# A second buffer for the routed rows, a drain with its own order, and the projection's bias on GpSimd, in layer 1's attention

## The reference, cut to what matters

```python
def _L1_attn_ref(x, ...):
    ...                                   # local windows and global tokens
    mix = sigmoid(concat([local, glob]) @ gate_w + gate_b)
    out = mix * local + (1.0 - mix) * glob
    return out @ out_w + out_b            # the projection and its bias

x = x + ga * _L1_attn_ref(h, ...)         # ga: one row of 128 for each batch
h = _layernorm(x) * (1 + cb) + sb         # the rows that are routed
gout = h @ Wgate + bgate
topv, topi = top_k(gout, 2)               # each token goes to two of 8 experts
topw = softmax(topv)
x = x + gb * _L1_ffn_ref(h, ...)
```

## Time and profile before

| | |
|---|---|
| median of 3 runs | 1575.2 us (1570.2 to 1600.82) |
| profiled execution | 1568.51 us |
| its span on the core | 1566.7 us |
| mean granted TensorE clock | 0.872 |
| TensorE busy | 1236.0 us (79%) |
| VectorE busy | 883.0 us (56%) |
| GpSimd busy | 597.6 us (38%) |
| ScalarE busy | 488.4 us (31%) |

### The profile page before, as it was taken

The page is one execution under the profiler, slowest core; times in us unless marked ns, Lnnn a source line. Parts: engine busy times, 40 slices in busy tenths (PEclk is TensorE's granted clock), DMA queues, the critical chain, the costliest instruction groups (busy, mean ns, idle before and its releaser), DMA issues.

```text
span 1566.7 us, 21243 instructions
## 1 busy us (share of the span) xinstructions
PE 1236.0 (79%) x7028; PEld 722.2 (46%) x7028; DVE 883.0 (56%) x2210; ACT 488.4 (31%) x1089; POOL 597.6 (38%) x628
## 2 busy tenths in 40 slices
PE   2677777777775469965999999999993289999991
PEld 1334444444443246643456556555562145555550
DVE  3556877877875412224346666666643345656655
ACT  0222222222221135540333443344330034444340
POOL 1335654665544415554113253444235202122221
PEclk9899989988986579995799998899985599999996
DMA  6001011011011152221011111200011151111105
GB/s 260 21 0 36 21 56 36 22 55 36 28 42 44 37 212 82 77 75 58 9 30 48 33 37 41 62 22 27 27 33 34 51 155 35 34 35 36 39 21 169
DMA packets 95138, 85.25 MB, mean 54 GB/s; under 512 B 10393, under 2 KB 87578, under 8 KB 94122
## 3 DMA queue, kind: packets, MB, share of 16 engines
q1 hardware_dynamic: 86074, 65.41, 13.9%
q0 software_dynamic: 8704, 17.97, 3.6%
q10 hardware_dynamic: 256, 0.53, 0.1%
HBM read 55.40 MB, written 30.07 MB: 55 GB/s over the span
## 4 chain that ended last, share of the span: by engine, by line
PE 45%; DVE 3%; issue 3%; POOL 2%; DMA 2%; ACT 1%; SPq 1%; POOLq 0%; DVEq 0%; ACTq 0%
PE bank L1692 8%; PE bank L1934 4%; PE bank L1678 4%; PE bank L1877 3%; PE bank L1831 3%; PE bank L1702 2%; PE bank L1884 2%; PE bank L1914 2%; PE bank L1843 2%; PE bank L1903 2%; PE bank L1916 2%; PE bank L1686 2%; POOL slots L1065 1%; PE bank L1899 1%; PE bank L1948 1%
## 5 line engine op out<-in xcount | busy, mean ns | idle before, releaser
L1065 POOL DMA_INDIRECT slots<-pay,slot x128 | 134.4, 1050 | 114.9 <-issue 89.3
L1582 PE MATMUL bank<-consts,region 128*128 128x128 f32 x512 | 82.0, 310 | 110.6 <-POOL region L1102 110.6
L1080 POOL DMA_INDIRECT y<-region,xin x80 | 76.6, 958 | 195.5 <-ACT region L1309 175.2
L1582 PEld LDWEIGHTS bank<-consts,region 128*128 128x128 f32 x512 | 72.2, 214 | 156.0 <-POOL region L1102 129.0
L1692 PE MATMUL bank<-wgl,rows 128*128 x288 | 139.0, 606 | 5.8 <-ACT rows L1292 5.8
L1102 POOL TENSOR_TENSOR region<-region 128x512 f32<-128x512 f32 x64 | 83.8, 1310 | 140.5 <-DVE region L779 111.1
L913 DVE TENSOR_REDUCE rows<-bank 128x4 f32<-128x512 f32 x128 | 79.5, 683 | 84.4 <-PE bank L1831 84.4
L1292 ACT ACTIVATE rows<-bank 128x256 f32<-128x256 f32 x216 | 80.8, 382 | 102.5 <-PE bank L1686 101.5
L1080 POOL DMA_INDIRECT y<-hh,region x64 | 61.3, 957 | 117.6 <-ACT hh L1309 102.9
L640 DVE TENSOR_TENSOR rows<-bank,w0uv 128x512 f32<-128x512 f32 x72 | 49.7, 691 | 95.8 <-PE bank L1692 87.3
L1428 ACT ACTIVATE w0uv<-bank 128x512 f32<-128x512 f32 x128 | 66.1, 603 | 86.7 <-PE bank L1884 86.7
(11 more groups left out here) (306 smaller groups left out, 2660.9 us busy)
## 6 DMA issues: line engine op xcount, KB each, us to landing
xin<-slots SPq DMA_DIRECT2D x80, 65.0 KB, 1.9
region<-slots SPq DMA_DIRECT2D x64, 65.0 KB
xres<-x SPq DMA_DIRECT2D x16, 256.0 KB, 2.3
wgl<-in_wgl SPq DMA_DIRECT2D x1, 4096.0 KB, 14.3
rows<-y SPq DMA_DIRECT2D x8, 512.0 KB, 4.1
wgl<-y SPq DMA_DIRECT2D x8, 512.0 KB, 7.5
wgl<-in_x SPq DMA_DIRECT2D x8, 256.0 KB, 3.0
w0uv<-in_w0uv SPq DMA_DIRECT2D x1, 2048.0 KB
```

The costliest lines, as they stand in the source:

```text
L1065: p.indirect_dma_start(io["slots"], bass.IndirectOffsetOnAxis(ap=slot[:, k, t:t + 1], axis=0), pay[:, k, t, :], None).then_inc(S["scattere ...
L1080: p.indirect_dma_start(io["y"], bass.IndirectOffsetOnAxis(ap=xins[par][:, h, k, P + 1:P + 2].bitcast(U32), axis=0), bYs[par][:, h, k, :], ...
L1582: ins = M(bank[7][:, tile(t)], pr[:, j % 2, tile(t)], center, start=(j == 0 and t == 0), stop=(j == DH - 1 and t == NT - 1), skip_group_ch ...
```

## The change

- `pay`, `h2` and `slot` get a second copy. In layer 1 batch b uses copy b % 2; layer 0 uses copy 0 alone. `modulate(b)` in layer 1 waits until the scatter of batch b - 2 has landed (`pay_free` at NB + b, at least NB + 1), where it waited for that of b - 1.
- Steps 8 to 10 are replaced by one function `tail(t)` with t = 7 on each engine, that does the same work for the batches 5, 6 and 7 in another order. The transposes and router products of batches 6 and 7 get banks of their own (`h2_bank`, `route_bank`), so that their waits for other users of banks 4 and 5 go.
- The four products with `ones1` are removed from layer 1's projection. `obg` now holds the gated bias on all 128 partitions, and `gated_out` adds it to the rows `X` with a GpSimd operation of 128x512. `outb` is loaded broadcast over the partitions. `residual` waits for that addition.
- `maxl` now lies over weights that only layer 0 uses. Its clearing moves from the program's start to the start of layer 1's attention, and the clearing of `ones1` goes.

```diff
+        def pay_of(layer, b):
+            return pays[b % 2 if layer else 0]
@@ attention_rows
-            for i in range(-2, NB + 3):
+            for i in range(-2, NB):
                 step(i)
+            tail(LAST)
@@ VectorE
-            V.memset(ones1[:, :], 1.0).then_inc(S["prep_v"], 1)
-            V.memset(maxl[:, :, :], 0.0).then_inc(S["prep_v"], 1)
@@ residual(b)
-                v.wait_ge(S["load_k"], 32 * b + 32)
+                v.wait_ge(S["c_owg"], 3 * b + 3)
@@ modulate(b)
-                v.wait_ge(S["pay_free"], NB + b + 1)
+                v.wait_ge(S["pay_free"], max(NB + 1, NB + b))
@@ VectorE
+            def tail(t):
+                norm_local(t, 1, 1)
+                modulate(t - 1)
+                router(1, t - 2, 0.0, 0)
+                router(1, t - 2, 0.0, 1)
+                mix(t, t % 2)
+                place(1, t - 2)
+                residual(t)
+                router(1, t - 1, 0.0, 0)
+                router(1, t - 1, 0.0, 1)
+                place(1, t - 1)
+                modulate(t)
+                router(1, t, 0.0, 0)
+                router(1, t, 0.0, 1)
+                place(1, t)
@@ GpSimd, gated_out(b)
-                G_.tensor_tensor(obg[:, :], outb[:, :], mrow[0:1, M_GA, :], ALU.mult).then_inc(S["c_owg"], 1)
+                G_.tensor_tensor(obg[:, :], outb[:, :], mrow[:, M_GA, :], ALU.mult).then_inc(S["c_owg"], 1)
+                p.wait_ge(S["c_owg"], 3 * b + 2)
+                G_.tensor_tensor(X, X, bc(obg[:, :], NT, 1), ALU.add).then_inc(S["c_owg"], 1)
@@ GpSimd
+            def tail(t):
+                gated_out(t)
+                difference(t, t % 2)
+                scatter(1, t - 2, 0)
+                scatter(1, t - 2, 1)
+                ln_scale("ln2_st", "ln2_rs", t + NB)
+                normalise("c_xh2", t)
+                scattered(1, t - 2)
+                for b in (t - 1, t):
+                    scatter(1, b, 0)
+                    scatter(1, b, 1)
+                    scattered(1, b)
@@ TensorE, project
-            def project(out, src, layer):
+            def project(out, src):
                 for t in range(NT):
-                    ins = M(out[:, tile(t)], src[:, tile(t)], owg[:, :], start=True, stop=layer == 0)
-                    if layer == 1:
-                        ins = M(out[:, tile(t)], ones1[:, :], obg[:, :], start=False, stop=True)
+                    ins = M(out[:, tile(t)], src[:, tile(t)], owg[:, :], start=True, stop=True)
@@ TensorE, out(b)
-                t_.wait_ge(S["c_owg"], 2 * b + 2)
+                t_.wait_ge(S["c_owg"], 3 * b + 1)
@@ TensorE
+            def tail(t):
+                attend_local(t, 1, 1)
+                turn_out(t, 0)
+                route(t - 2)
+                turn_out(t, 1)
+                h2_T(t - 1)
+                gate(t, t % 2)
+                rank(1, t - 2)
+                out(t)
+                route(t - 1)
+                rank(1, t - 1)
+                h2_T(t)
+                route(t)
+                rank(1, t)
```

130 lines of the change are left out of this document (84 added, 46 removed).

## The result

| | before | after |
|---|---|---|
| median, us (4 runs each) | 1588.0 | 1548.7 |
| the runs, us | 1570.2, 1575.2, 1600.8, 1604.7 | 1547.9, 1548.5, 1548.9, 1552.0 |
| ratio, 95% interval | | 0.985 (0.982 to 0.989) |
| profiled execution, us (span) | 1568.5 (1566.7) | 1548.9 (1547.0) |
| mean granted clock | 0.872 | 0.874 |

The change makes the kernel faster, by 1.5% with an interval of 0.4% to either side. The profiled pair differs by 19.6 us, the medians by 39.3. Such an interval can be too narrow: in a later group of runs the kernel before, compared with itself on one chip, came out at 0.989 (0.982 to 0.996).

What follows compares the result with a forecast made beforehand. TensorE's queue was taken to bound layer 1's attention, then a drain of 81 us waiting on buffer and scatters. 9.9 + 15.3 + 0.5 = 25.7 us gave 1542.8 or 1549.5, stated as 1545, range 1531 to 1556.

Steps and rivals of the forecast that it cites:

- The chances: Whole kernel: 0.66 for a change within 2%, 0.32 for over 2% faster, 0.02 for over 2% slower.
- the sum of 25.7 us: Whole kernel: gains of 9.9 us in main steps, 15.3 in the drain and 0.5 at the start.
- Bias products, main steps: Layer 1's `out(b)`: removing length-1 products saves 1.66 us each, about 1.4 kept in four steps; 9.9 us in all.
- TensorE keeps its clock more often: Rival, main steps: two half-clock stretches of about 10 us vanish, 7 us more gained, 1536 us; chance 0.17.
- The row that spoke for it: Evidence for the clock rival: both long half-clock stretches, 10.1 and 9.9 us, begin at the removed bias products.
- The objection: Against the clock rival: in the fifth and last steps the clock falls 3 us after those products, in `attend_local`.
- The addition on GpSimd: One 128x512 addition per batch, 1.26 us, off the path: 0 us, bound 8.8; lock rival 1551 us, chance 0.07.
- The drain: After the last main step: `scatter(7)` begins at 1213.8 instead of 1229.11, limited by GpSimd's queue; 15.3 us gained.
- the order: Drain's new sequence of batches 5 to 7: counted as 2.5 us less on VectorE, within the drain's gain.
- The start: Program start: two clearings ahead of TensorE's first product go, so it starts 0.5 us earlier.
- The wait moves: Rival: bias products were hidden (9.9 falls to 3) or drain stays scatter-bound (15.3 to 8); 1550 us, chance 0.13.
- Slower: Rival, main steps: without filler products TensorE sits at half clock longer, 75 us more cancelling the gain; chance 0.03.

Runs made afterwards that it cites:

- grouped: Kernel before with layer 1's four length-1 bias products behind the four length-128 ones instead of between them; 1559.5 us, ratio 0.977.
- doubled: Changed kernel with the projection's four products made twice in each batch; 1558.8 us (ratio 0.973), in a later group 1541.9 us (0.965).
- the one of 1602.2 us: Profiled execution of the unaltered kernel before, its second run in the last group on a third chip; that run's median 1599.9 us.
- first and fourth profile: Changed kernel, nothing altered: profiled in the original comparison (median 1548.7 us) and again as yardstick of the fourth group (1544.0 us, ratio 0.966).
- the third buffer: Changed kernel with a third buffer for batch 7's rows and slots and GpSimd's drain queue reordered, no landing awaited between scatters; 1597.8 us, ratio 0.996.
- the first group: Experiments on the change's parts one by one, mostly on the kernel before, whose median there was 1594.8 us (13 runs).

## Why the forecast was right and where it was wrong

**The chances.** 0.66 was put on a change within 2%, as about what a measurement can tell. The step that failed is this equation of "under 2%" with "no change". The comparison's interval is 0.4% to either side (0.3 to 0.8% in the later ones), so the ratio of 0.985 stands clear of one, no two runs overlap, and the sum of 25.7 us, 1.64%, was itself a change of that size. The kernel before against itself, 1.1% off at worst, says that not much under 1.5% could be told. In later groups the ratio was 0.993, 0.985 and 0.966: the size belongs to chip and spell. The sign was the same each time; in the group with 0.993 the runs overlap, and it isn't certain there.

**The time.** 1545 was forecast, 1548.7 measured, inside the range. That agreement is partly luck, as the terms show. The forecast also took its start from an execution of 1568.5 us, near the fastest that the kernel before has, so it says little of the 39 us between the medians.

**Bias products, main steps (9.9 us).** The price of 1.66 us was too low, half of 3.33: removing them gives 2.34, because the alternation alone costs 1.16. The limit on what is kept was found at the right place, but `attend_local` behind `norm_global` was named for the last step only (0.95 us there, 0.82 measured), and the exponentials not at all. Kept is 1.2 to 1.4 us a step (51.17 us before without half clock, 50.0 grouped, 49.8 doubled; the changed kernel has no such step), where 1.40 was forecast. Two errors cancel. The profiled pair doesn't show the 9.9 us: from the stage's first `global_values` (727.08 and 727.63) to the mark it gives only 2.0 us. In part that is because the changed kernel spent 84.9 us there at half clock instead of 76.7 (3.4 more ahead of the first `out`, and 13.7 instead of none between `out(5)` and `out(6)`), which at 0.4 us lost per us is some 3 us; the rest isn't traced.

**TensorE keeps its clock more often (0.17, two stretches, 7 us).** In the profiled pair it doesn't: the two stretches at `out` are gone, but others came. Of the medians this rival is the best account why they stand 39 us apart and not 20 (the two executions of 1601 and 1605 us left no trace, but the kernel before has such ones in every group), and there it was underweighted. The row that spoke for it, both stretches beginning at the products that go, was right. The objection, that two others began 3 us behind them in `attend_local`, concerned 3.4 us stretches, such as every kernel has; they begin 4.4 and 2.3 us behind the products, in `again_local`. Its price was taken from the execution of 1568.5 us. In the one of 1602.2 us it is 4 times 8.5 us or more. The rule cited from the Trainium skill, page "TensorE: Matmul & The Clock Gate", section "What's actually happening", that the window runs free of the kernel, would let the stretches fall by chance. Within one kernel executions do differ by up to 36 us, which agrees; and the changed kernel's first and fourth profile have eight stretches each from 840 to 1140 us, seven of which differ by the same 0.45 us, which doesn't speak against it. But chance alone would not put 21 of 25 long falls at the same place in the step.

**The addition on GpSimd (0 us).** Right; VectorE is held for 0.9 us (1.57 instead of 0.69) in one place, and without that meeting the time is the same. The rule cited from the Trainium skill, page "SBUF — State Buffer", section "SBUF: two separate sides", agrees with that row, whose operation has two inputs in SBUF (the VectorE operation in the earlier trace rows lists one, so it wasn't an example of the two-input case). Six of the seven additions in the main steps run beside VectorE's maxima from PSUM, which keep their 0.68 us each, as the forecast had it.

**The drain (15.3 us).** 16.8 us from mark to `scatter(7)`. Each forecast moment came 2.8 to 3.2 us early (`out(7)` 1183.2 and 1180.4, `normalise(7)`'s end 1200.6 and 1197.5, `scatter(7)` 1213.8 and 1210.9), 1.45 us of that from the main steps. The limit, GpSimd's queue with one landing in it, is confirmed by the third buffer, which shortens it by 2.2 us and finds the padding next. What the forecast didn't see is that the order, 2.5 us of its sum, is worth nothing: the buffer alone gives it all, 20.3 us from mark to `scatter(7)` in its profile.

**The start (0.5 us).** Nothing. Without the clearings VectorE is 0.67 us faster, but the loads that it waits for landed 0.74 us later, and the first product starts at 15.60 instead of 15.53.

**The wait moves (0.13).** It does in part: 1.2 of the 2.34 us of the first main step go to VectorE and ScalarE, but that share had never been in the sum.

**Slower (0.03).** Not so in the time. More time at half clock, its premise, is there in the profiled pair, 8 us of it and not 75; the longest times at half clock are those of kernels with the filler products or with late exponentials.

**Left open.** Why a run of alternating products is followed by long half-clock stretches in some executions and 10 us ones in others; what holds ScalarE's exponentials in the steps that scatter (the releaser is outside the profile); what holds back the padding writes with the third buffer; and how much of the 39 us is the alternation's alone: grouping, which takes only it away, gave 35 us in the medians of the first group, from 13 and 4 executions.

## What to carry to other kernels

Price a removed instruction by a kernel or stage without it, not by its share of the records: here products of unlike length cost more in alternation than their sum, and grouping them got the same gain with no other change. Compare a kernel with itself before reading a difference of a per cent. When the executions of a kernel differ by 2%, profile one from the upper end as well before weighing a clock rival. Ahead of an order of one's own for a drain, try the buffer alone.

## What the hardware showed beyond that

- Four products with contraction length 128 and four with length 1: 3.33 us alternating, 2.17 us grouped, 0.99 us for the four long ones alone, at full clock.
- TensorE fell to 1.2 GHz for 23.9 us with no idle time in its records ahead of it, four times, each time within 0.5 us of the end of such an alternating run. One microsecond at half clock cost 0.42 us there (8.54 us over 20.5).
- ScalarE's exponentials were held beside indirect scatters by amounts that repeat (0.65, 1.4, 2.1, 2.8, 3.6 and 4.3 us, once 5.7), on one chip in all four profiles, on another in the three of one group and in no other.
- A VectorE multiplication of 128x512 with both inputs in SBUF took 1.57 us beside a GpSimd addition of 1.26 us, and 0.69 us alone; VectorE's maxima from PSUM took 0.68 us with and without it.
- Four plain DMA issues on ScalarE's queue took 2.61 us among the eight issues of one scatter, and 8.97 us where 24 scatters were issued with no landing awaited between them.
